# A decoder block on one core: four feed-forward products moved into the last attention batch, turns three units ahead

## The chip, the core and the metric

The kernel runs as one program on one core of a Trainium2 chip. TensorE (PE, with its weight loads listed apart as PEld), VectorE (DVE), ScalarE (ACT) and GpSimd (POOL) work side by side; SyncE (SP) issues the DMAs. Each engine takes its instructions in order, and the engines wait for one another by semaphores only. What counts is the device time of one execution in microseconds, as the median of several runs.

## What is computed

32 sequences of 56 tokens, 128 wide, pass through one decoder layer: linear self-attention, cross-attention (16 heads of 8) over a context of 1500 rows per sequence, and a feed-forward net, each with a residual and a layer norm. The change touches only the seam between cross-attention and feed-forward net:

```python
x = _layernorm(x + attn(x, ...))                    # LN1
x = _layernorm(x + xattn(x, ctx_1024, ctx_1024, ...))   # LN2, gives x2
hidden = x2 @ W1 + b1                               # 128 -> 512
imag   = w_imag * sin(theta + hidden * 0.1)
q      = hidden + (cos(theta)*w_real + sin(theta)*w_imag) * imag * 0.1
x = _layernorm(x2 + relu(q) @ W2 + b2)              # LN3
```

## The kernel before

The first 140 us hold the self-attention and the first norm. Then 32 batches of cross-attention follow (`body` on each engine), two to a pass of a loop, the last two written out by hand. A batch has 12 tiles of 125 context rows (`KT`), in six steps of two tiles, 2m and 2m+1. In a step PE multiplies queries and keys (`score`, line 1066, into banks 0 to 2, in turn by half tiles), ACT takes the exponential of each half (`exp`, line 756), and PE multiplies by the values (`pv`, lines 1083 and 1089, summed in bank 7). Between these, PE prepares the next batches (keys, values, row maxima) in four ring banks, 3 to 6. In the last batch (`not s2`) there is no next batch: the ring is empty but for `x2_T` in steps 2, 4 and 6 (by tile), which transposes the normed rows of quads 0 to 2 into bank 5, from where ACT copies them into `x2T` (line 830). A quad is 8 sequences, 512 columns.

The feed-forward net works in 16 units k, quad q = k // 4 by hidden slice g = k % 4, each 128 x 512 in float32. One unit passes through four engines:

- `hidden(k)`, PE line 1147: the product with W1, into bank g. It waits until `modulated(k - 4)` has read that bank (`z_ready`).
- `turn(k)`, ACT line 843: scale and bias, to turns of the sine, PSUM to SBUF.
- `rounded(k)`, DVE line 1446: the nearest whole number; then POOL line 696 subtracts it (the fraction).
- sine, ACT line 851 (behind one table load, since the last batch used the exponential).
- `modulated(k)`, DVE line 1452: sine times a coefficient plus the product in bank g; `relu(k)`, DVE line 1459; `project(k)`, PE line 1158: the product with W2.

The order on each engine is written out by hand. ACT: sine(k), then turn(k + AHEAD). DVE: modulated(k), rounded(k + AHEAD), relu(k), and between them the rest of the last pair of batches (`normalise_o` line 1336, `turn_o` line 1342, `add_y` line 1347, whose PE parts are the end units T line 982, Z line 986, Y line 989), the statistics and the norm of the last quad (`normalised(0, LAST)`, line 1394, behind the root on POOL, lines 542 and 545) and, at k = 6, 10 and 14, the sum and the statistics of a finished quad (`sum3`, lines 1465, 1379, 1385). PE: hidden(k), then project(k - 5). The turns, the whole numbers, the sines and the modulated values have four buffers each (`FBUF`). POOL does the 16 fractions in order, with the root of the last quad behind fraction 4 (`ROOT_UNIT`).

Before, no unit starts until the last exponential is through: PE waits for `p_ready` of all batches, then issues hidden(0), hidden(1). The lines that set this:

```python
AHEAD = 2
X2T_BANK, F_BANKS = banks[5], (banks[4], banks[7])
for k in range(AHEAD):
    turn(k)                                         # ACT, behind the last exponential
pe.wait_ge(p_ready, B * 2 * KT)                     # PE, ahead of hidden(0)
wait_past(pe, z_ready, k - G + 1)                   # in hidden(k): G = 4 banks
```

Of the kernel before, what the change touches and what calls it, by code (L numbers as in the profile page):

```python
# [33 lines left out]
ALU = mybir.AluOpType  # L34
# [3 lines left out]
P = 128  # L38
# [8 lines left out]
G = 4  # L47
# [39 lines left out]
def wait_past(engine, semaphore, count):  # L87

    if not isinstance(count, int) or count > 0:
        engine.wait_ge(semaphore, count)  # L90
# [10 lines left out]


STORE_ORDER = (0, 1, 3, 2)
END_SLOT = 3
END_UNITS = {2: "T", 4: "Z", 5: "Y"}
X2T_STEPS = (2, 4, 6)
FBUF = 4
PROJECT_LAG = 5
AHEAD = 2
ROOT_UNIT = 4  # L110
EARLY_M = 7
U1_SHIFT = 3
# [129 lines left out]
def decoder_block(nc, ctx_dram, x_dram, pack_dram, out_dram, m):  # L242
# [6 lines left out]
    with ExitStack() as stack:  # L249
# [112 lines left out]
        LAST = QUADS - 1  # L362
        W1, W2 = w("W1"), w("W2").rearrange("p (g n) -> p g n", g=G)
        out_view = out_dram.rearrange("(q p e) n d -> q e n p d", q=QUADS, e=2)
        X2T_BANK, F_BANKS = banks[5], (banks[4], banks[7])

        scores = banks[0:RING_AT]
        ring = banks[RING_AT:RING_AT + RING]
# [5 lines left out]
        with nc.Block() as block:  # L374
# [330 lines left out]
            def _(act):  # L705
# [121 lines left out]

                def x2_T(q):
                    act.wait_ge(x2T_ps, q + 1)
                    nc.scalar.copy(x2T[:, q, :], X2T_BANK).then_inc(x2T_sb, 1)  # L830

                for b in range(2):
                    body(b, b % 2, True, True)
# [6 lines left out]

                def turn(k):
                    act.wait_ge(h_ps, k + 1)
                    nc.scalar.activation(turns[:, k % FBUF, :], banks[k % G], ACT.Identity,
                                         bias=u_bias[:, k % G:k % G + 1], scale=0.1 * INV2PI).then_inc(turns_ready, 1)

                for k in range(AHEAD):
                    turn(k)
                for k in range(UNITS):
                    act.wait_ge(frac_ready, k + 1)
                    wait_past(act, z_ready, k - FBUF + 1)  # L850
                    nc.scalar.activation(sine[:, k % FBUF, :], turns[:, k % FBUF, :], ACT.Sin,
                                         scale=TWO_PI_BELOW).then_inc(sine_ready, 1)
                    if k + AHEAD < UNITS:
                        turn(k + AHEAD)
                    if k == ROOT_UNIT + 2:
                        x2_T(LAST)

            @block.tensor
            def _(pe):
# [197 lines left out]
                def score(b, t, u):  # L1057
                    if t == 0:
                        pe.wait_ge(k_stacked, (b + 1) * 96)
                        pe.wait_ge(qd_ready, b + 1)  # L1060
                        pe.wait_ge(m_placed, (b + 1) * 64)
                    wait_past(pe, p_ready, b * 2 * KT + 2 * t - 1)
                    for g in range(G):
                        for half in range(2):
                            rows = slice(HALF * half, HALF * half + HALF)
                            mm = nc.tensor.matmul(scores[(2 * t + half) % RING_AT][:, g * PAIR:(g + 1) * PAIR],  # L1066
                                                  k_stack[u][rows, g, t * KP:t * KP + P],
                                                  q_diag[u][rows, g * PAIR:(g + 1) * PAIR], start=True, stop=True)
                            if g == G - 1:
                                mm.then_inc(s_ready, 1)  # L1070
# [26 lines left out]
                def body(b, pair, u, s1, s2, before, held):  # L1097

                    held = dict(held)

                    def go(units):
                        for kind, i in units:
                            if active(kind, s1, s2, before):
                                n, slot = of_batch(kind, b, pair), slots[u][kind, i]
                                if kind in ("M1", "M2") and i in PAIRS:
                                    release(held[slots[u][kind, i + 1]])
                                unit(kind, i, n, u if kind in ("K2", "M2") else 1 - u, ring[slot], held[slot])
                                held[slot] = (kind, i, n)

                    for m, (one, two, three) in enumerate(plans[u]):  # L1110
                        score(b, 2 * m, u)
                        if not s2 and 2 * m in X2T_STEPS:
                            x2_T(X2T_STEPS.index(2 * m))
                        go(one)
                        score(b, 2 * m + 1, u)
                        go(two)
                        if m:
                            pv(b, 2 * m - 2, u)
                            pv(b, 2 * m - 1, u)
                        elif before:  # L1120
                            pv(b - 1, KT - 2, 1 - u)
                            pv(b - 1, KT - 1, 1 - u)
                        go(three)
                    if not s2:
                        pv(b, KT - 2, u)
                        pv(b, KT - 1, u)
# [6 lines left out]
                def x2_T(q):  # L1133

                    pe.wait_ge(x2_done, q + 1)
                    wait_past(pe, x2T_sb, q)
                    for p in range(4):
                        last = nc.tensor.transpose(X2T_BANK[:, p * P:(p + 1) * P], x_all[:, q, p * D:(p + 1) * D],
                                                   ident)
                    last.then_inc(x2T_ps, 1)  # L1140

                def hidden(k):
                    q, g = divmod(k, G)
                    if g == 0:
                        pe.wait_ge(x2T_sb, q + 1)
                    wait_past(pe, z_ready, k - G + 1)
                    nc.tensor.matmul(banks[g], W1[:, g * P:(g + 1) * P], x2T[:, q, :], start=True,
                                     stop=True).then_inc(h_ps, 1)

                def project(k):  # L1150
# [25 lines left out]
                pe.wait_ge(p_ready, B * 2 * KT)  # L1176
                for k in range(UNITS + PROJECT_LAG):
                    if k in END_UNITS:
                        unit(END_UNITS[k], 0, B // 2 - 1, 0, ring[END_SLOT], None)
                    if k == ROOT_UNIT + 5:  # L1180
                        x2_T(LAST)
                    if k < UNITS:
                        hidden(k)
                    if k >= PROJECT_LAG:
                        project(k - PROJECT_LAG)

            @block.vector
            def _(dve):
# [151 lines left out]
                def turn_o(pair, bank):  # L1340
                    dve.wait_ge(ready["Z"], pair + 1)
                    dve.tensor_copy(oT[:, :], bank[:, 0:P]).then_inc(oT_done, 1)
# [89 lines left out]
                with dve.Fori(1, B // 2 - 1) as i:  # L1432
                    for u in range(2):
                        body(i * 2 + u, i, u, True, True, True)
                body(B - 2, B // 2 - 1, 0, False, True, True)
                o_copy(B - 2, 0)
                invert_std(0, early, 1)
# [2 lines left out]
                body(B - 1, B // 2 - 1, 1, False, False, True)  # L1440


                def rounded(k):
                    dve.wait_ge(turns_ready, k + 1)
                    wait_past(dve, frac_ready, k - FBUF + 1)
                    dve.tensor_scalar(whole[:, k % FBUF, :], turns[:, k % FBUF, :], ROUND, -ROUND, ALU.add,
                                      ALU.add).then_inc(whole_ready, 1)

                def modulated(k):

                    dve.wait_ge(sine_ready, k + 1)
                    dve.scalar_tensor_tensor(z[:, k % FBUF, :], sine[:, k % FBUF, :], s_coef[:, k % G:k % G + 1],  # L1452
                                             banks[k % G], ALU.mult, ALU.add).then_inc(z_ready, 1)

                def relu(k):
                    dve.wait_ge(z_ready, k + 1)
# [5 lines left out]
                def sum3(q):  # L1462
# [5 lines left out]
                    stats_of(1, pairs)  # L1468
                    variances(1, pairs, q + 1)

                last_pair, last_quad = B // 2 - 1, range(4 * LAST, 4 * QUADS)
                o_copy(B - 1, 1)
                for k in range(AHEAD):
                    rounded(k)
                normalise_o(last_pair, ring[END_SLOT])
                for k in range(UNITS):
                    modulated(k)
                    if k + AHEAD < UNITS:
                        rounded(k + AHEAD)
                    relu(k)  # L1480
                    if k == 0:
                        turn_o(last_pair, ring[END_SLOT])
                    if k == 1:
                        add_y(last_pair, ring[END_SLOT])
                    if k == 2:
                        dve.wait_ge(y_added, last_pair + 1)
                        stats_of(0, last_quad)
                        variances(0, last_quad, 2)
                    if k == ROOT_UNIT:
                        invert_std(0, last_quad, 2)  # L1490
                        normalised(0, LAST).then_inc(x2_done, 1)
                    if k >= G + 2 and k % G == 2:
                        sum3(k // G - 1)
# [51 lines left out]
```

## Time and profile before

| what | us |
|---|---|
| median of 3 runs (lowest, highest) | 752.18 (751.29, 757.26) |
| the profiled execution | 756.2 |
| its span, first to last instruction | 754.4 |
| last batch and feed-forward net, from the last batch's first scores | 690.4 to 754.4 |

The profile shows one execution, 4.0 us above the median; its span is 1.8 us shorter than its time. Times of rows are microseconds from the span's start. A row of the timeline has start, duration, engine, line, operation, output <- inputs by the program's names, shapes and a count; in brackets stands how long the engine was idle before it and what ended that wait. A row of windows has the stretch, its length, the busy time of PE, PEld, DVE, ACT and POOL with instruction counts, the granted clock of TensorE as a share of 2.4 GHz, the share of the DMA engines and GB/s. The tiles have other names in the rows where memory is reused: `e_buf` holds the turns, `c_in` the whole numbers, the two `k_stack` the sines and the modulated values, `kf` is `x2T`, `qf` and `probs` take the results of `relu`, `pack` holds the weights.

### The profile page before, as it was taken

How to read it: one execution, taken by the hardware profiler on the slowest of the kernel's cores; microseconds unless marked ns; L12 is line 12 of the kernel's file. 1: busy time of each engine (PE TensorE's matmuls, PEld its weight loads, DVE VectorE, ACT ScalarE, POOL GpSimd, SP SyncE). 2: the span in 40 equal slices, each digit the busy share in tenths (PEclk: the TensorE clock that was granted, in tenths of full speed). 3: DMA queues.
4: the chain of work that ended last, by engine and by line, in shares of the span. 5: the costliest groups of instructions: out<-in, count | busy, mean ns of one | idle time of the engine just before them, and what ended most of it. 6: DMA issues, size and time to landing. Idle time of an engine off the chain costs nothing.

```text
span 754.4 us, 33172 instructions
## 1 busy us (share of the span) xinstructions
PE 677.6 (90%) x12468; PEld 436.7 (58%) x12468; DVE 586.4 (78%) x1139; ACT 549.5 (73%) x1123; POOL 470.6 (62%) x507
## 2 busy tenths in 40 slices
PE   6879865897899999999999999999999999997883
PEld 3556432554566666666666666666666666665552
DVE  3768866776687888888888887788888788885597
ACT  3537522786688888888888888888888888887751
POOL 6526424366467777777777767776777777723464
PEclk9989976799999999999999999999999999999997
DMA  7202502587758778888777877877787877851001
GB/s 215 82 2 93 95 1 65 82 161 171 146 120 161 147 144 151 158 161 176 149 146 157 152 151 152 151 151 143 149 159 166 170 150 144 140 108 21 1 1 49
DMA packets 39405, 93.20 MB, mean 124 GB/s; under 512 B 7880, under 2 KB 14536, under 8 KB 39368
## 3 DMA queue, kind: packets, MB, share of 16 engines
q1 hardware_dynamic: 39368, 92.69, 60.7%
q8 instruction: 25, 0.41, 0.3%
q14 instruction: 12, 0.10, 0.1%
HBM read 66.06 MB, written 26.54 MB: 123 GB/s over the span
## 4 chain that ended last, share of the span: by engine, by line
PE 68%; DVE 14%; issue 7%; ACT 6%; DMA 2%; SPq 1%; POOL 1%; ACTq 0%; DVEq 0%; POOLq 0%
PE psum L974 13%; PE psum L1066 13%; PE psum L1083 11%; PE psum L962 9%; PE psum L1089 8%; DVE mx L1313 4%; PE psum L954 4%; ACT probs L756 3%; PE psum L905 2%; DMA q_diag<-mT 1%; DVE rden L1241 1%; PE psum L891 1%; PE psum L920 1%; PE psum L982 1%; DVE k_stack L1452 1%
## 5 line engine op out<-in xcount | busy, mean ns | idle before, releaser
L1313 DVE TENSOR_REDUCE mx<-psum 128x1 f32<-128x500 f32 x672 | 424.3, 673 | 96.6 <-PE psum L974 94.5
L756 ACT ACTIVATE probs<-psum 125x448 f32<-125x448 f32 x768 | 376.2, 544 | 82.5 <-PE psum L1066 80.7
L974 PE MATMUL psum<-kh,q_max 64*128 64x500 f16 (+1 forms) x672 | 149.4, 385 | 12.5 <-DVE mx L1313 11.3
L1066 PE MATMUL psum<-q_diag,k_stack 64*128 64x112 f16 x3072 | 143.3, 212 | 12.6 <-issue 3.0
L1083 PE MATMUL psum<-probs,v_ext 125*32 125x112 f32 x3072 | 149.1, 266 | 0.0
L1089 PE MATMUL psum<-probs,v_ext 125*32 125x112 f32 x3072 | 144.3, 260 | 0.0
L580 POOL CAST kh<-k 128x500 f16<-128x500 f32 x96 | 57.7, 601 | 132.8 <-ACT k L776 125.1
L1066 PEld LDWEIGHTS psum<-q_diag,k_stack 64*128 64x128 f16 x3072 | 87.7, 95 | 88.2 <-ACT probs L756 50.5
L568 POOL TENSOR_TENSOR c_hl<-c_in,c_hl 128x500 f16<-128x500 f32 x96 | 109.9, 1145 | 7.7
L586 POOL TENSOR_TENSOR kl<-k,kh 128x500 f16<-128x500 f32 x96 | 107.3, 1146 | 0.0
L1083 PEld LDWEIGHTS psum<-probs,v_ext 125*32 125x32 f32 x3072 | 74.0, 109 | 35.9 <-issue 31.0
L1089 PEld LDWEIGHTS psum<-probs,v_ext 125*32 125x32 f32 x3072 | 87.2, 111 | 0.0
L566 POOL CAST c_hl<-c_in 128x500 f16<-128x500 f32 x96 | 59.4, 619 | 37.6 <-PE psum L962 35.2
L974 PEld LDWEIGHTS psum<-kh,q_max 64*128 64x128 f16 (+1 forms) x672 | 38.5, 94 | 67.4 <-issue 30.6
L962 PE MATMUL psum<-WvH,c_hl 128*128 128x128 f16 x768 | 76.0, 221 | 0.0
L962 PE MATMUL psum<-WvL,c_hl 128*128 128x128 f16 x384 | 69.8, 220 | 3.1 <-issue 3.1
L776 ACT ACTIVATE k<-psum,pack 128x500 f32<-128x500 f32 x96 | 65.1, 679 | 8.9 <-PE psum L954 7.6
L962 PEld LDWEIGHTS psum<-WvH,c_hl 128*128 128x128 f16 x768 | 58.2, 98 | 23.1 <-DVE mx L1313 15.4
L765 ACT COPY v_ext<-psum 125x512 f32<-125x512 f32 x96 | 56.4, 588 | 4.0 <-PE psum L962 4.0
L954 PE MATMUL psum<-c_hl,WkH 128*128 128x500 f16 x192 | 57.0, 378 | 0.4 <-ACT mT L771 0.4
L607 POOL TENSOR_TENSOR q_max<-qh,pack 128x896 f16<-128x896 f32 (+1 forms) x32 | 54.0, 1689 | 1.4 <-ACT qh L747 1.4
L726 ACT ACTIVATE e_buf<-psum 128x512 f32<-128x512 f32 x32 | 19.6, 611 | 28.4 <-PE psum L891 24.9
(143 smaller groups left out, 705.9 us busy)
## 6 DMA issues: line engine op xcount, KB each, us to landing
k_stack<-k_halves SPq DMA_DIRECT2D x192, 187.5 KB, 6.3
c_in<-ctx_in SPq DMA_DIRECT2D x32, 750.0 KB, 5.3
k_halves<-kh SPq DMA_DIRECT2D x32, 375.0 KB, 5.9
k_halves<-kl SPq DMA_DIRECT2D x32, 375.0 KB, 6.3
q_stack<-q_halves SPq DMA_DIRECT2D x32, 64.0 KB, 2.4
q_diag<-mT SPq DMA_DIRECT2D x64, 0.8 KB
q_diag<-mT SPq DMA_DIRECT2D x64, 0.1 KB
out<-x_all SPq DMA_DIRECT2D x8, 112.0 KB
```

Source lines behind the costliest of these rows:

```text
L566: nc.gpsimd.tensor_copy(c_hl[:, buf, 0, keys], c_in[:, buf, keys]).then_inc(c_hi, 1)
L568: nc.gpsimd.tensor_tensor(c_hl[:, buf, 1, keys], c_in[:, buf, keys], c_hl[:, buf, 0, keys], ALU.subtract).then_inc(c_split, 1)
L586: nc.gpsimd.tensor_tensor(kl[u][:, keys], k32[:, keys], kh[u][:, keys], ALU.subtract).then_inc(kl_done, 1)
L756: nc.scalar.activation(probs[0:KP, t % PBUF, half * 2 * GC:(half + 1) * 2 * GC], scores[k % RING_AT][0:KP, 0:2 * GC], ACT.Exp, scale=SCALE ...
L776: nc.scalar.activation(k32[:, i * CH:(i + 1) * CH], bank[:, 0:CH], ACT.Identity, bias=w("bk")).then_inc(k32_done, 1)
L954: last = nc.tensor.matmul(bank[:, 0:CH], wt[:, :], c_hl[:, u, part, i * CH:(i + 1) * CH], start=(k == 0), stop=(k == 2))
L962: last = nc.tensor.matmul(bank[:, j * P:(j + 1) * P], c_hl[:, u, part, at:at + P], wt[:, :], start=(k == 0), stop=(k == 2))
L974: last = nc.tensor.matmul(bank[:, 0:CH], q_max[u][rows, r * P:(r + 1) * P], kh[u][rows, c * CH:(c + 1) * CH], start=True, stop=True)
L1066: mm = nc.tensor.matmul(scores[(2 * t + half) % RING_AT][:, g * PAIR:(g + 1) * PAIR], k_stack[u][rows, g, t * KP:t * KP + P], q_diag[u][ro ...
L1083: nc.tensor.matmul(O[32 * j:32 * j + 32, 0:2 * N], v_ext[u][0:KP, v:v + 32], probs[0:KP, t % PBUF, at:at + 2 * N], start=(t == 0), stop=(t ...
L1089: last = nc.tensor.matmul(O[32 * j:32 * j + 32, 2 * N:GC], v_ext[u][0:KP, v:v + 32], probs[0:KP, t % PBUF, at + 2 * N:at + GC], start=Fals ...
L1313: dve.tensor_reduce(mx[:, r * KC + c:r * KC + c + 1], bank[:, 0:CH], AX.X, ALU.max).then_inc(mx_done, 1)
```

## The change

In the last batch PE now issues hidden(0) and hidden(1) in the step of tile 6, behind x2_T, hidden(2) in the step of tile 8 and hidden(3) in that of tile 10, each ahead of the step's second score. The products of all units go to the ring's banks 3 to 6 instead of banks 0 to 3. The turns of units 0 to 3 are made by DVE (`first_turn`) instead of ACT, each followed by its `rounded`, ahead of the last copy of O; POOL's order is as before, so its fractions 0 to 3 come as soon as those are there. In the rest of the net a turn runs three units ahead of its sine instead of two. The transposes of the last quad, the results of `project` and the end units move to other banks.

```diff
-END_SLOT = 3
-AHEAD = 2
+AHEAD = 3
+PREPARED = 4
+PREPARED_AT = {6: (0, 1), 8: (2,), 10: (3,)}
...
-        X2T_BANK, F_BANKS = banks[5], (banks[4], banks[7])
+        X2T_BANKS, F_BANKS, END_BANK = (banks[5], banks[2]), (banks[0], banks[1]), banks[7]
...
-                    nc.scalar.activation(turns[:, k % FBUF, :], banks[k % G], ACT.Identity,
+                    nc.scalar.activation(turns[:, k % FBUF, :], banks[3 + k % G], ACT.Identity,
...
-                for k in range(AHEAD):
-                    turn(k)
                 for k in range(UNITS):
...
-                    if k + AHEAD < UNITS:
+                    if PREPARED <= k + AHEAD < UNITS:
                         turn(k + AHEAD)
...
                         go(one)
+                        if not s2 and 2 * m in PREPARED_AT:
+                            for k in PREPARED_AT[2 * m]:
+                                hidden(k)
                         score(b, 2 * m + 1, u)
...
-                        unit(END_UNITS[k], 0, B // 2 - 1, 0, ring[END_SLOT], None)
+                        unit(END_UNITS[k], 0, B // 2 - 1, 0, END_BANK, None)
...
-                    if k < UNITS:
+                    if PREPARED <= k < UNITS:
                         hidden(k)
...
+                def first_turn(k):
+                    dve.wait_ge(h_ps, k + 1)
+                    dve.tensor_scalar(turns[:, k, :], banks[3 + k % G], 0.1 * INV2PI, u_bias[:, k % G:k % G + 1],
+                                      ALU.mult, ALU.add).then_inc(turns_ready, 1)
...
+                for k in range(PREPARED):
+                    first_turn(k)
+                    rounded(k)
                 last_pair, last_quad = B // 2 - 1, range(4 * LAST, 4 * QUADS)
                 o_copy(B - 1, 1)
-                for k in range(AHEAD):
-                    rounded(k)
-                normalise_o(last_pair, ring[END_SLOT])
+                normalise_o(last_pair, END_BANK)
                 for k in range(UNITS):
                     modulated(k)
-                    if k + AHEAD < UNITS:
+                    if PREPARED <= k + AHEAD < UNITS:
                         rounded(k + AHEAD)
                     relu(k)
```

PE in the last batch, from x2_T of quad 2 (line 1138) to the score of tile 8, before. Line 1066 is a score of one tile, lines 1083 and 1089 are products with the values.

```order
L1138 MATMUL psum<-pack,x_all 128x128 x4
L1066 MATMUL psum<-q_diag,k_stack 128x112 x8
L1083 MATMUL psum<-probs,v_ext 32x112 x4
L1089 MATMUL psum<-probs,v_ext 32x112 x4
L1083 MATMUL psum<-probs,v_ext 32x112 x4
L1089 MATMUL psum<-probs,v_ext 32x112 x4
L1066 MATMUL psum<-q_diag,k_stack 128x112 x16
```

The same place in the changed kernel, whose lines there are x2_T 1140, hidden 1149, score 1065, pv 1082 and 1088:

```order
L1140 MATMUL psum<-pack,x_all 128x128 x4
L1149 MATMUL psum<-kf,pack 128x512 x2
L1065 MATMUL psum<-q_diag,k_stack 128x112 x8
L1082 MATMUL psum<-probs,v_ext 32x112 x4
L1088 MATMUL psum<-probs,v_ext 32x112 x4
L1082 MATMUL psum<-probs,v_ext 32x112 x4
L1088 MATMUL psum<-probs,v_ext 32x112 x4
L1065 MATMUL psum<-q_diag,k_stack 128x112 x8
L1149 MATMUL psum<-kf,pack 128x512
L1065 MATMUL psum<-q_diag,k_stack 128x112 x8
```

Two products stand between x2_T and the score of tile 7, and one between the two scores of the next step.

DVE behind the norm of quads 0 to 2 (line 1394), before: the copy of O (1351), two roundings (1446), the reciprocal and the product of `normalise_o`, then modulated(0) (1452), rounded(2), relu(0) (1459), the copy for Y (1342), modulated(1).

```order
L1394 TENSOR_SCALAR x_all<-x_all,mv_f,rstd_f 128x128 x12
L1351 COPY o_sb<-psum 128x4x56
L1446 TENSOR_SCALAR c_in<-e_buf 128x512 x2
L1329 RECIPROCAL r_tok<-psum 128x16
L1336 TENSOR_TENSOR o_tok<-psum,r_tok 128x2x4x8 x2
L1452 SCALAR_TENSOR_TENSOR k_stack<-k_stack,s_coef,psum 128x512
L1446 TENSOR_SCALAR c_in<-e_buf 128x512
L1459 TENSOR_SCALAR qf<-k_stack,pack 128x512
L1342 COPY oT<-psum 128x128
L1452 SCALAR_TENSOR_TENSOR k_stack<-k_stack,s_coef,psum 128x512
```

The same place in the changed kernel, from the last first_turn (1445) and its rounded (1440), of which three more such pairs stand ahead:

```order
L1445 TENSOR_SCALAR e_buf<-psum,u_bias 128x512
L1440 TENSOR_SCALAR c_in<-e_buf 128x512
L1353 COPY o_sb<-psum 128x4x56
L1331 RECIPROCAL r_tok<-psum 128x16
L1338 TENSOR_TENSOR o_tok<-psum,r_tok 128x2x4x8 x2
L1459 SCALAR_TENSOR_TENSOR k_stack<-k_stack,s_coef,psum 128x512
L1466 TENSOR_SCALAR qf<-k_stack,pack 128x512
L1344 COPY oT<-psum 128x128
L1459 SCALAR_TENSOR_TENSOR k_stack<-k_stack,s_coef,psum 128x512
L1440 TENSOR_SCALAR c_in<-e_buf 128x512
```

The roundings 0 to 3 now stand ahead of the copy of O, and rounded(4) stands directly behind modulated(1), one unit earlier than before.

## Rows read from the trace of the kernel before

**Rows 1.** The page's busy time of each engine, share of the span, instructions.

```profile
PE 677.6 (90%) x12468; PEld 436.7 (58%) x12468; DVE 586.4 (78%) x1139; ACT 549.5 (73%) x1123; POOL 470.6 (62%) x507
```

**Rows 2.** Windows: the seam, units 0 to 4, units 5 to 15.

```profile
703.20:708.40 5.20, 4.79 (x37) 2.29 (x29) 2.55 (x7) 3.34 (x5) 1.95 (x2) 1.00 0.00 0
708.40:720.10 11.70, 9.12 (x46) 5.92 (x45) 11.67 (x30) 7.47 (x13) 8.87 (x8) 1.00 0.00 1
720.10:744.90 24.80, 18.97 (x114) 14.22 (x114) 22.86 (x58) 10.59 (x18) 16.97 (x12) 0.99 0.00 1
```

**Rows 3.** Timeline of the last batch: scores, products with values, exponentials, then hidden(0), hidden(1).

```profile
697.15 0.37 PE L1066 MATMUL psum<-q_diag,k_stack 64*128 64x112 f16 x8
...
697.88 3.02 ACT L756 ACTIVATE probs<-psum 125x448 f32<-125x448 f32 x6
...
699.51 0.37 PE L1066 MATMUL psum<-q_diag,k_stack 64*128 64x112 f16 x8 [0.63 <-ACT probs L756]
...
699.82 0.40 PE L1083 MATMUL psum<-probs,v_ext 125*32 125x112 f32 x8
...
700.72 0.37 PE L1066 MATMUL psum<-q_diag,k_stack 64*128 64x112 f16 x8
701.13 1.98 ACT L756 ACTIVATE probs<-psum 125x448 f32<-125x448 f32 x4 [0.23 <-PE psum L1066]
...
703.70 1.98 PE L1147 MATMUL psum<-kf,pack 128*128 128x512 f32 x4
```

**Rows 4.** Timeline of the seam.

```profile
703.84 0.39 DVE L1351 COPY o_sb<-psum 128x224 f32<-128x224 f32 x1 [8.81 <-PE psum L1089]
...
704.86 0.69 ACT L843 ACTIVATE e_buf<-psum,u_bias 128x512 f32<-128x512 f32 x1 [1.75 <-PE psum L1147]
...
705.52 0.60 PE L982 MATMUL psum<-pack,o_sb 128*128 128x128 f32 x4
...
706.42 1.28 ACT L851 ACT_TABLE_LOAD   x1
...
707.55 0.25 DVE L1329 RECIPROCAL r_tok<-psum 128x16 f32<-128x16 f32 x1
...
707.72 0.63 ACT L851 ACTIVATE k_stack<-e_buf 128x512 f32<-128x512 f32 x1
707.84 0.35 DVE L1336 TENSOR_TENSOR o_tok<-psum,r_tok 128x64 f32<-128x64 f32 x2
...
708.38 0.75 DVE L1452 SCALAR_TENSOR_TENSOR k_stack<-k_stack,s_coef,psum 128x512 f32<-128x512 f32 x1 [0.19 <-ACT k_stack L851]
```

**Rows 5.** Timeline: a rounding while POOL stands still, then one full unit.

```profile
725.68 0.42 DVE L1446 TENSOR_SCALAR c_in<-e_buf 128x512 f32<-128x512 f32 x1
...
728.33 0.75 DVE L1452 SCALAR_TENSOR_TENSOR k_stack<-k_stack,s_coef,psum 128x512 f32<-128x512 f32 x1
...
728.99 0.73 DVE L1446 TENSOR_SCALAR c_in<-e_buf 128x512 f32<-128x512 f32 x1
...
729.64 0.47 DVE L1459 TENSOR_SCALAR qf<-k_stack,pack 128x512 f32<-128x512 f32 x1
729.80 1.45 POOL L696 TENSOR_TENSOR e_buf<-e_buf,c_in 128x512 f32<-128x512 f32 x1 [0.36 <-DVE c_in L1446]
```

**Rows 6.** Timeline: POOL's root and fractions 5 and 6, DVE's norm of the last quad.

```profile
714.77 0.23 POOL L542 TENSOR_SCALAR std_f<-mv_f 128x4 f32<-128x4 f32 x1 [0.15 <-DVE mv_f L1385]
...
716.09 1.27 POOL L696 TENSOR_TENSOR e_buf<-e_buf,c_in 128x512 f32<-128x512 f32 x1
...
717.72 1.44 POOL L696 TENSOR_TENSOR e_buf<-e_buf,c_in 128x512 f32<-128x512 f32 x1 [0.36 <-DVE c_in L1446]
...
717.96 2.06 DVE L1394 TENSOR_SCALAR x_all<-x_all,mv_f,rstd_f 128x128 f32<-128x128 f32 x4
```

**Rows 7.** Windows of the net's end, and a float32 product of 128 x 512 at 0.50.

```profile
744.00:746.00 2.00, 0.54 (x5) 0.33 (x3) 1.09 (x5) 0.00 (x0) 0.87 (x1) 0.59 0.00 0
...
130.03 2.07 PE L940 MATMUL psum<-x1T,pack 128*128 128x512 f32 x2 [0.68 <-ACT x1T L743]
```

More of the change, by code:

```diff
@@ L829, in x2_T @@
                     act.wait_ge(x2T_ps, q + 1)
-                    nc.scalar.copy(x2T[:, q, :], X2T_BANK).then_inc(x2T_sb, 1)
+                    nc.scalar.copy(x2T[:, q, :], X2T_BANKS[q // LAST]).then_inc(x2T_sb, 1)
                 for b in range(2):
@@ L1137, in x2_T @@
                     for p in range(4):
-                        last = nc.tensor.transpose(X2T_BANK[:, p * P:(p + 1) * P], x_all[:, q, p * D:(p + 1) * D],
-                                                   ident)
+                        last = nc.tensor.transpose(X2T_BANKS[q // LAST][:, p * P:(p + 1) * P],
+                                                   x_all[:, q, p * D:(p + 1) * D], ident)
                     last.then_inc(x2T_ps, 1)
@@ L1146, in hidden @@
                     wait_past(pe, z_ready, k - G + 1)
-                    nc.tensor.matmul(banks[g], W1[:, g * P:(g + 1) * P], x2T[:, q, :], start=True,
+                    nc.tensor.matmul(banks[3 + g], W1[:, g * P:(g + 1) * P], x2T[:, q, :], start=True,
                                      stop=True).then_inc(h_ps, 1)
@@ L1434, in _, with rounded @@
                         body(i * 2 + u, i, u, True, True, True)
+                def rounded(k):
+                    dve.wait_ge(turns_ready, k + 1)
+                    wait_past(dve, frac_ready, k - FBUF + 1)
+                    dve.tensor_scalar(whole[:, k % FBUF, :], turns[:, k % FBUF, :], ROUND, -ROUND, ALU.add,
+                                      ALU.add).then_inc(whole_ready, 1)
+                def first_turn(k):
+                    dve.wait_ge(h_ps, k + 1)
+                    dve.tensor_scalar(turns[:, k, :], banks[3 + k % G], 0.1 * INV2PI, u_bias[:, k % G:k % G + 1],
+                                      ALU.mult, ALU.add).then_inc(turns_ready, 1)
                 body(B - 2, B // 2 - 1, 0, False, True, True)
@@ L1440, in _ @@
                 body(B - 1, B // 2 - 1, 1, False, False, True)
[L1443 to L1447, printed above, removed]
                 def modulated(k):
@@ L1452, in modulated @@
                     dve.scalar_tensor_tensor(z[:, k % FBUF, :], sine[:, k % FBUF, :], s_coef[:, k % G:k % G + 1],
-                                             banks[k % G], ALU.mult, ALU.add).then_inc(z_ready, 1)
+                                             banks[3 + k % G], ALU.mult, ALU.add).then_inc(z_ready, 1)
                 def relu(k):
@@ L1481, in _ @@
                     if k == 0:
-                        turn_o(last_pair, ring[END_SLOT])
+                        turn_o(last_pair, END_BANK)
                     if k == 1:
-                        add_y(last_pair, ring[END_SLOT])
+                        add_y(last_pair, END_BANK)
                     if k == 2:
```

## The prediction

> **What bounds the kernel now.** I read the busy times first: PE leads with 90% of the span, DVE follows with 78% [rows 1]. That average says little here, since the change touches only the last 64 us. So I cut that stretch into windows [rows 2]. In the seam, from the last exponential to the first modulated unit, DVE works 2.55 of 5.20 us and POOL 1.95: everybody waits in turn. In units 0 to 4 DVE is busy for 11.67 of 11.70 us, and in units 5 to 15 for 22.86 of 24.80, most of the rest being one wait for a root at the end. So the last batch is an ACT matter, the seam a chain of latencies, the net a DVE matter.
>
> In the last batch, ACT runs six exponentials without a gap (697.88, 3.02 us), then four more after a wait of 0.23 [rows 3]. A step of two tiles takes it 1.98 + 0.23 = 2.21 us. PE in the same step gives 0.31 us to each score (699.51 to 699.82) and 0.90 to the values of two tiles (699.82 to 700.72): 1.52 us, so 0.69 us are spare.
>
> The seam is read along the waits [rows 4]. The last exponential ends at 703.11 (701.13 + 1.98). hidden(0) is issued at 703.70, its turn starts 1.16 us later, the second turn follows, then the table load at 706.42, the first sine at 707.72 and modulated(0) at 708.38, which the row says waited for that sine. From the last exponential to modulated(0) that is 5.27 us.
>
> A steady unit [rows 5]: modulated 0.75, rounded 0.73, relu 0.47, and POOL's fraction 1.45 us, starting 0.36 after the one before it ended, so every 1.81 us. The rounding takes 0.42 us when POOL stands still, and 0.73 when a fraction runs: it ends only when POOL has finished. This ring (fraction, then the next rounding, then the next fraction) sets 1.81 us, not DVE's own sum, 0.67 + 0.35 + 0.40 = 1.42 us from start to start with the starts overlapped by some 0.08.
>
> **The change part by part.** *Products in the last batch.* Four rows of line 1147, two products, start at 703.70 and the next PE work starts at 705.52 [rows 3, 4]: 0.91 us each. Two of them stand ahead of the score of tile 7, which was issued at 697.15. It moves to 698.97, and an exponential starts 0.41 us behind its score (700.72 to 701.13), so at 699.38. That exponential started at 697.88 before: 1.50 us late. In each of the next two steps PE now has 1.52 + 0.91 = 2.43 us against ACT's 2.21, 0.22 each. Sum: +1.9 us at the last exponential. Bounds: 0, if PE's spare time hides all of it, and 4 x 0.91 = 3.6, if none. I take 1.9, since it is the sum of steps that rows show.
>
> *The seam.* The turns of units 0 to 3 move to DVE, which waits 8.81 us ahead of the copy of O [rows 4]. A read of PSUM by DVE on this shape costs about what modulated does, 0.75 [rows 5]: 4 x (0.75 + 0.42) = 4.7 us, hidden by that wait, and the four fractions by an idle POOL. Without that cover the fourth pair would push the copy of O by 1.2 us. Behind the last exponential two chains remain. ACT: table load 1.28 and sine 0.63, 1.96 us with the small gaps. DVE and PE: the copy of O starts 0.73 after the exponential and takes 0.39, then T 0.60, the reciprocal 0.25, the product 0.35, with some 0.05 for each of four hand-overs: 2.5 us. The second ends last, so 5.27 becomes 2.5: -2.75 us. What is late next is the old rest of the attention, no longer the table load.
>
> One rule bears on this. In the row the sine starts 0.02 us after the table load has ended (706.42 + 1.28 = 707.70, then 707.72) [rows 4]. The Trainium skill (page "ScalarE: Activation LUTs", section "What ACT_TABLE_LOAD costs") adds a drain of about 1.38 us to each switch, 2.66 us in all. By the row ACT's chain is 1.96 us and hidden; by the rule it would be 3.34 and set the end, +0.85 on the sum. The trace shows no drain, so I go by the row and keep the rule as a rival.
>
> *Units 0 to 4, with turns three ahead.* DVE loses two roundings here, at 0.42 that is -0.84. But the turns gain a tighter loop. There are still four banks, so hidden(k + 3) waits for modulated(k - 1), where hidden(k + 2) waited for modulated(k - 2). From the end of modulated(0) to rounded(4): 0.1 for the hand-over, 1.16 to the turn, 0.69 for the turn [rows 4], 1.95 us in all. DVE has only relu(0), the copy for Y and modulated(1) meanwhile, 0.40 + 0.20 + 0.67 = 1.27 (the copy is an estimate from that of O, 0.39 for 224 columns [rows 4], at 128): it stands for 0.7 us in front of rounded(4), with relu(1) and all behind it, and much the same in front of rounded(7). POOL then adds to it. The root of the last quad stands behind fraction 4 and needs the statistics that DVE makes behind relu(2). With modulated(0) at 708.38 - 2.75 + 1.9 = 707.5, rounded(4) starts at 710.2, and relu(1), add_y, modulated(2), rounded(5), relu(2) and the statistics follow until 714.1. Then POOL does the root in 1.32 (714.77 to 716.09 [rows 6]) and fractions 5, 6 and 7, all of them waiting, at about 1.3, 1.3 and 1.45, until 719.5. Before, only two fractions stood ahead of the norm: fraction 6 ended at 719.16 and the norm at 720.02, 0.86 later. With one more the norm ends at about 720.4 to 720.7. I take 720.5: from modulated(0) this stretch grows from 11.65 to 13.0 us, +1.35. Bounds: -0.84, if nobody ever waits for a turn, and +2.5, if each of the turns 4 to 7 costs 0.7 and the roundings go at no gain.
>
> *Units 5 to 15.* In the steady stretch the new loop takes 1.95 + 0.42 + 0.40 + 0.67 = 3.44 us for two units, 1.72 each, under POOL's 1.81: nothing. Behind each of the first two sums, where POOL is idle and DVE could run a unit in 1.4 us, the loop costs some 0.2: +0.4. At the end the last rounding comes one unit earlier: -0.2. Sum +0.2. Bounds: -0.4, and +3.6 (the second rival).
>
> *Other banks, other places of the end units.* T, Z and Y now work in bank 7 and wait for the copy of O as before; project finds banks 0 and 1 free, since sine(0) follows the last exponential on ACT. No queue has a DMA moved. 0, with the sum of the seam as cover.
>
> **Sum.** 1.9 - 2.75 + 1.35 + 0.2 = +0.7 us. The profiled execution, 754.4 us of span and 756.2 in all, would become 755.1 and 756.9. It lies 4.0 us above the median of the runs, in what no part of this change touches, so I add the difference to the median: 752.18 + 0.7 = 752.9 us. A measurement of this kernel can tell about 1%, 7.5 us, from no change, so I expect a result that cannot be told from it.
>
> **The rivals.** *The head start stays.* If the turns three ahead never hold DVE, the gain of the seam remains: 1.9 - 2.75 - 0.84 - 0.4 = -2.1, 750.1 us. For it: in the steady unit POOL's ring, not the turn, decides. Against it: four banks, and a chain of 1.95 us where DVE has 1.27 to do.
>
> *The slower side: hidden stands behind project.* PE takes its products in order. If hidden(k + 3) regularly finds project(k - 3) just started, it waits up to 0.9 us more, the chain grows from 1.95 to 2.85 and a unit to (2.85 + 1.49) / 2 = 2.15 us against 1.81. Over 11 units that is +3.6, 756.5 us. It decides from the point where relu and modulated free the two products at the same moment. Against it: project of a unit is released four units earlier, so it normally runs right behind the hidden before it.
>
> *The clock falls in the seam.* The granted clock fell towards 0.50, 1.2 GHz, at 744 to 746, with PE busy for 0.54 of 2 us [rows 7]. With four products gone, PE has little but T, Z and Y for some 2.5 us. A float32 product of this shape took 2.07 at 0.50 [rows 7], against 1.0 in the net; two units of hidden and project slower by some 1.8 each would be +3.6, 756.5. Against it: the clock was 1.00 through the stretch with similar pauses in units 0 to 4 [rows 2].
>
> *The drain of the page.* +0.85 more: 753.8. *The change does not do what it says:* the prepared units are not finished when the batch ends, so that the 1.9 us remain and about half of the seam's gain goes: 754.3.
>
> **How the numbers follow.** Forecast 0.55, head start 0.18, project 0.12, clock 0.07, drain 0.04, not prepared 0.04. The range is 749.5 to 757.0: the low end is the first rival less 0.6 us for the scatter of runs, the high end the second and third with 0.5 more. The forecast's own range is 751.5 to 755. None of the cases is 1% faster, 744.7: 0.02. Project and clock together would reach 760, over 759.7: 0.04. Within 1%: 0.94.
>
> **What would show it.** Right: the last exponential ends some 1.9 us later, with the gap in front of the exponentials of tile 7; the table load follows the last exponential at once; modulated(0) starts about 2.5 us behind it, waiting for the product of normalise_o; DVE stands some 0.7 us in front of rounded(4), by ACT's turn; three fractions run without a pause behind the root. Wrong: no wait for turns in units 4 to 7, roundings at 0.42 in the steady units, units longer than 1.81 us, or a granted clock under 1.00 between 705 and 740.

## The result: one part in a hundred slower by the medians, two microseconds slower where the change works

The changed kernel took 764.91 us, median of 5 runs (758.77 to 765.63), against 757.26 for 5 runs of the kernel before: the 3 shown above and two more, 762.66 and 1824.48. The ratio is 1.0111 with an interval of 1.0065 to 1.0157. The ratios here and below leave out runs over 1.5% above the fastest of their kernel, with them some of the plain scatter (4 of 12 runs of e3_ahead2, 1 of 12 of e2_after_again), while the medians hold all runs. Forecast were 752.9 us, in a range of 749.5 to 757.0. The profiled execution took 758.77 us, its span 757.0, 2.6 us more than before.

The two traces allow a sharper comparison. Take the copy of O of the batch before the last as zero (DVE line 1351 before, 1353 after, at 690.51 and 691.15): it lies ahead of everything that the change touches. From there to the end of DVE's last instruction it is 61.05 us before and 62.98 after, **+1.93 us**. The other 0.64 us of the spans' difference arose earlier, where the change edits nothing.

The last batch after, from the timeline (lines 1149 hidden, 757 exponentials; compare [rows 3]):

```profile
697.08 0.66 PE L1140 MATMUL psum<-pack,x_all 128*128 128x128 f32 x4
697.58 1.88 PE L1149 MATMUL psum<-kf,pack 128*128 128x512 f32 x4
...
699.39 0.37 PE L1065 MATMUL psum<-q_diag,k_stack 64*128 64x112 f16 x8
...
699.80 0.98 ACT L757 ACTIVATE probs<-psum 125x448 f32<-125x448 f32 x2 [1.16 <-PE psum L1065]
...
702.36 0.98 ACT L757 ACTIVATE probs<-psum 125x448 f32<-125x448 f32 x2 [0.38 <-PE psum L1065]
...
704.93 0.98 ACT L757 ACTIVATE probs<-psum 125x448 f32<-125x448 f32 x2 [0.38 <-PE psum L1065]
```

The score of tile 7 stands behind two products, and ACT waits 1.16 us for it; behind each of the later two products ACT waits 0.38 us. The last exponential ends at 705.91 (704.93 + 0.98), 2.16 us later against the zero point than before.

The seam, of the same timeline (compare [rows 4]):

```profile
705.93 1.28 ACT L850 ACT_TABLE_LOAD   x1
...
706.64 0.39 DVE L1353 COPY o_sb<-psum 128x224 f32<-128x224 f32 x1 [0.79 <-PE psum L1088]
...
707.17 0.63 PE L981 MATMUL psum<-pack,o_sb 128*128 128x128 f32 x4 [0.60 <-DVE o_sb L1353]
707.22 1.15 ACT L850 ACTIVATE k_stack<-e_buf 128x512 f32<-128x512 f32 x2
...
708.13 0.35 DVE L1338 TENSOR_TENSOR o_tok<-psum,r_tok 128x64 f32<-128x64 f32 x2
708.40 0.74 DVE L1459 SCALAR_TENSOR_TENSOR k_stack<-k_stack,s_coef,psum 128x512 f32<-128x512 f32 x1
```

From the last exponential to modulated(0) it is now 2.49 us instead of 5.27. The sines are ready early; the copy of O, T and normalise_o decide.

Units 1 to 4, of the same timeline (compare [rows 6]):

```profile
711.14 0.43 DVE L1440 TENSOR_SCALAR c_in<-e_buf 128x512 f32<-128x512 f32 x1 [0.62 <-ACT e_buf L844]
...
715.06 0.23 POOL L543 TENSOR_SCALAR std_f<-mv_f 128x4 f32<-128x4 f32 x1 [1.96 <-DVE mv_f L1387]
...
716.38 4.12 POOL L697 TENSOR_TENSOR e_buf<-e_buf,c_in 128x512 f32<-128x512 f32 x3
...
717.54 0.43 DVE L1440 TENSOR_SCALAR c_in<-e_buf 128x512 f32<-128x512 f32 x1 [0.54 <-ACT e_buf L844]
...
717.88 1.50 DVE L1466 TENSOR_SCALAR probs<-k_stack,pack 128x512 f32<-128x512 f32 x1
...
719.30 2.05 DVE L1396 TENSOR_SCALAR x_all<-x_all,mv_f,rstd_f 128x128 f32<-128x128 f32 x4
```

DVE waits 0.62 us in front of rounded(4) and 0.54 in front of rounded(7), both for ACT's turn. POOL stands still for 1.96 us in front of the root, then does three fractions in a row, 4.12 us, and DVE's relu(4) takes 1.50 instead of 0.48 beside them; the norm takes 2.05, as before. The norm ends at 721.35, 12.95 us behind modulated(0), where it was 11.64.

Then the clock. From the windows after (the columns as in [rows 2], the granted clock third from the end), and the timeline:

```profile
718.00:720.00 2.00, 1.42 (x10) 0.99 (x8) 2.00 (x2) 1.53 (x3) 2.00 (x2) 1.00 0.00 0
720.00:722.00 2.00, 0.59 (x4) 0.42 (x4) 2.00 (x6) 0.00 (x0) 0.50 (x1) 0.95 0.00 0
722.00:724.00 2.00, 2.00 (x4) 0.91 (x4) 1.40 (x4) 0.00 (x0) 1.44 (x1) 0.50 0.00 0
724.00:726.00 2.00, 2.00 (x11) 1.76 (x10) 1.10 (x3) 1.69 (x3) 0.60 (x1) 0.70 0.04 8
```

```profile
722.06 2.07 PE L1149 MATMUL psum<-kf,pack 128*128 128x512 f32 x2
...
724.17 0.69 ACT L844 ACTIVATE e_buf<-psum,u_bias 128x512 f32<-128x512 f32 x1 [4.40 <-PE psum L1149]
...
724.89 0.43 DVE L1440 TENSOR_SCALAR c_in<-e_buf 128x512 f32<-128x512 f32 x1 [1.50 <-ACT e_buf L844]
```

PE was busy for 0.59 of 2 us while the norm of the last quad ran. Then the granted clock is 0.50, 1.2 GHz, from about 722 to 725. hidden(9) takes 2.07 instead of 1.1 us, its turn comes late, and DVE stands for 1.50 us in front of rounded(9). Before, hidden(9) ran at 720.73, and the clock was 1.00:

```profile
720.00:722.00 2.00, 1.93 (x9) 1.21 (x10) 2.00 (x6) 0.99 (x2) 0.91 (x1) 1.00 0.00 0
...
720.73 1.13 PE L1147 MATMUL psum<-kf,pack 128*128 128x512 f32 x2
```

### The profile page after: what moved, and what is told of

The parts are those of the page before. It is cut to its first block, busy times and chain, and to the rows that moved or that the text cites. A ratio compares the mean times of both kernels' runs of the same rounds, so it can differ in the third digit from the quotient of the medians.

```text
span 757.0 us, 33172 instructions
## 1 busy us (share of the span) xinstructions
PE 681.2 (90%) x12468; PEld 438.3 (58%) x12468; DVE 588.7 (78%) x1143; ACT 547.7 (72%) x1119; POOL 470.5 (62%) x507
## 4 chain that ended last, share of the span: by engine, by line
PE 70%; DVE 13%; issue 7%; ACT 6%; DMA 2%; SPq 1%; POOL 0%; ACTq 0%; DVEq 0%; POOLq 0%
PE psum L973 13%; PE psum L1065 13%; PE psum L1082 11%; PE psum L961 9%; PE psum L1088 8%; DVE mx L1315 5%; PE psum L953 4%; ACT probs L757 3%; PE psum L904 2%; PE psum L1149 2%; PE psum L890 1%; DVE rden L1243 1%; DMA q_diag<-mT 1%; PE psum L981 1%; PE psum L888 1%
```

## The experiments

All were timed in later sessions; where a ratio is given, it is against runs of the kernel before in the same comparison. The distances are differences of timeline rows of each profile, from the copy of O of the batch before the last (zero) to the end of the last exponential, the start of modulated(0), the end of the last quad's norm, the start of the first sum (k = 6) and the end of DVE's work, in us.

| kernel | last exponential | modulated(0) | norm | first sum | end |
|---|---|---|---|---|---|
| before | 12.60 | 17.87 | 29.51 | 32.63 | 61.05 |
| e1_before_again | 12.59 | 17.87 | 29.50 | 32.61 | 61.04 |
| after | 14.76 | 17.25 | 30.20 | 34.48 | 62.98 |
| e2_after_again | 14.75 | 17.24 | 30.19 | 34.47 | 62.96 |
| e3_ahead2 | 14.76 | 17.25 | 28.00 | 31.12 | 59.54 |
| e4_fill | 14.75 | 17.24 | 30.19 | 33.53 | 62.02 |
| e5_five_banks | 14.76 | 17.25 | 29.52 | 32.64 | 60.67 |
| e6_root_later | 14.77 | 17.26 | 29.21 | 32.54 | 61.01 |
| e7_prep2_ahead2 | 13.30 | 15.79 | 27.77 | 30.89 | 59.32 |
| e8_before_ahead3 | 12.59 | 19.21 | 32.90 | 36.36 | 64.84 |
| e9_prep3_ahead2 | 13.89 | 16.38 | 27.57 | 30.68 | 59.12 |
| e10_five_root | 14.76 | 17.25 | 28.51 | 31.62 | 59.64 |

**Both kernels again.** No edit.

> The kernel before, unchanged, timed against itself. Theory A (the scatter of runs carries most of the 7.65 us between the two medians; the change itself costs about 2 us, as the two profiles show from the last batch on): the interval of the ratio holds 1.000 and is some 0.005 wide or more on each side. Theory B (the change costs 7 to 8 us in most executions, which the one profile, the fastest of its runs, does not show): the ratio is 1.000 within 0.003, so that 1.011 cannot be scatter.

> The changed kernel, unchanged, once more. Theory A: ratio near 1.002 to 1.004, and from the last batch's first score to the end of DVE again about 63.1 us against 61.2. Theory B: ratio near 1.011 again, and in a slower execution a longer net, by a granted clock under 1.00 in more of it than 721.9 to 725.3. My theory before the result (turns three ahead eat the gain of the seam): the last exponential 2.2 us late, modulated(0) 2.5 us behind it, the stretch from there to the norm's end 12.9 us.

Measured: the kernel before against itself 1.0021 (0.9983 to 1.0059), median 758.68 of 12 runs; the changed kernel 1.0000 (0.9965 to 1.0034), median 759.2 of 12 runs, beside 758.33 for 35 runs of the kernel before, which lie between 752.15 and 764.19. Theory B falls with the second of these: the 1.011 of the first comparison did not come back. The first alone does not decide, since 1.0021 also lies within the 0.003 that theory B named. Theory A holds in that both intervals contain 1.000; they are a little narrower than it said, 0.0034 to 0.0038 to each side instead of 0.005, and 1.0000 is less than its 1.002 to 1.004. Its distances hold: two profiles of one kernel agree within 0.02 us over the last 61 to 63 us. Whether a slower execution has a longer net was not seen, since both profiles show quicker ones, 755.12 and 756.02 us. The ratio 1.0000 says less than it seems, since the interval is some 5 us wide; +1.93 us lies within it.

Where the scatter arises is seen in the distances between the copies of O of successive batches. From the fourth on they are 17.87 and about 17.1 us in turn, with few exceptions, up to the last one ahead of the zero point, which lies between 16.91 and 18.81. The first three were 18.65, 19.73 and 19.24 us in e10_five_root (749.09 us) and 19.38, 24.27 and 23.58 in e6_root_later (762.58 us). Their sum runs from 57.62 to 67.23 us over the twelve profiles; the first copy, ahead of them, comes at 153.34 to 157.52. Two windows and a PE row from the third of these distances, e10 first:

```profile
200.00:205.00 5.00, 2.99 (x60) 1.86 (x59) 2.17 (x5) 3.49 (x8) 3.14 (x4) 1.00 0.64 86
205.00:210.00 5.00, 4.83 (x120) 3.46 (x121) 3.68 (x6) 3.85 (x8) 2.00 (x3) 1.00 0.64 152
...
204.93 0.27 PE L963 MATMUL psum<-WvH,c_hl 128*128 128x128 f16 x2 [1.89 <-issue]
```

```profile
200.00:205.00 5.00, 2.96 (x67) 2.00 (x63) 3.08 (x6) 2.38 (x5) 3.47 (x4) 1.00 1.03 138
205.00:210.00 5.00, 2.90 (x19) 1.12 (x19) 0.78 (x2) 1.61 (x3) 0.00 (x0) 0.50 0.07 13
...
207.09 0.46 PE L1065 MATMUL psum<-q_diag,k_stack 64*128 64x112 f16 x5 [4.13 <-issue]
```

In the last row PE has stood for 4.13 us in the middle of a score. "issue" means that the profile shows nothing that it waited for; DVE and ACT wait for PE, for 4.99 and 4.83 us, POOL does nothing from 205 to 210, and PE goes on at a clock of 0.50. From 150 to 225 us such pauses of PE come to 4.7 us in e10 and to 10.4 in e6, and all twelve profiles have them. No part of the change is near. What makes PE pause, and longer in some executions than in others, was not tried and stays open.

**Turns two ahead.**

```diff
-AHEAD = 3
+AHEAD = 2
```

> The changed kernel with turns two ahead, as before; the four products stay in the last batch. If the loop of the turns is what eats the gain: from modulated(0) to the norm's end about 10.3 us, not 12.95, no wait of DVE in front of rounded(4) and rounded(7), the norm before the third waiting fraction; in all 2.5 to 3.5 us under the changed kernel and 1 to 2 us under the kernel before, ratio about 0.998. Rival (the loss comes from the products in the last batch and the clock, not from the turns): within 1 us of the changed kernel, and the clock falls at the same place.

Measured: 59.54, 3.44 us under the changed kernel and 1.51 under the kernel before; modulated(0) to the norm 10.75 us; median 754.21, ratio 0.9918 (0.9876 to 0.9960), of which the traces support 0.998. The rows of e3 where the changed kernel waited:

```profile
709.23 0.42 DVE L1440 TENSOR_SCALAR c_in<-e_buf 128x512 f32<-128x512 f32 x1
...
711.33 0.23 POOL L543 TENSOR_SCALAR std_f<-mv_f 128x4 f32<-128x4 f32 x1 [0.16 <-DVE mv_f L1387]
...
712.65 1.27 POOL L697 TENSOR_TENSOR e_buf<-e_buf,c_in 128x512 f32<-128x512 f32 x1
...
714.29 1.44 POOL L697 TENSOR_TENSOR e_buf<-e_buf,c_in 128x512 f32<-128x512 f32 x1 [0.36 <-DVE c_in L1440]
714.52 2.06 DVE L1396 TENSOR_SCALAR x_all<-x_all,mv_f,rstd_f 128x128 f32<-128x128 f32 x4
```

rounded(4) waits for nothing, two fractions stand between root and norm, and the clock stays at 1.00. So the turns three ahead, not the products in the last batch, cost the gain. The stretch came out 0.45 us longer than expected.

**PE kept busy in front of the transposes.** The two products' results are not used.

```diff
+FILL = 2
...
                     if k == ROOT_UNIT + 5:
+                        for _ in range(FILL):
+                            nc.tensor.matmul(X2T_BANKS[1], W1[:, 0:P], x2T[:, 0, :], start=True, stop=True)
                         x2_T(LAST)
```

> The changed kernel with two more products of 128 x 512 on PE in front of the transposes of the last quad, into a bank that these overwrite; their results are not used. If the pause of PE in front of the norm's end makes the clock fall: clock 1.00 from 720 to 726, hidden(9) at about 1.1 instead of 2.07 us, DVE's wait in front of rounded(9) down from 1.50 to some 0.5, 1 us gained from the norm's end on. Theory B in addition: the median falls by several us. Rival (the clock does not depend on this pause): hidden(9) again at 2.07, and no gain.

Measured: 62.02, 0.96 us less than the changed kernel, nearly all of it between norm and first sum (3.34 instead of 4.28 us). Windows of e4, and its rounded(9):

```profile
720.00:722.00 2.00, 1.74 (x7) 0.71 (x6) 2.00 (x7) 0.00 (x0) 0.08 (x1) 1.00 0.00 0
722.00:724.00 2.00, 2.00 (x12) 1.34 (x11) 1.45 (x4) 1.19 (x3) 1.45 (x1) 1.00 0.00 0
```

```profile
723.53 0.43 DVE L1443 TENSOR_SCALAR c_in<-e_buf 128x512 f32<-128x512 f32 x1 [0.55 <-ACT e_buf L845]
```

The clock is 1.00 and the wait 0.55, so the slow clock's price here is 0.96 us. The median did not fall (761.29, ratio 1.0033, 0.9997 to 1.0070), the last of theory B.

**Five banks; the root later; both.** Five banks for the products, so that hidden waits for one unit further back (turn, first_turn and modulated read the same five, and the transposes of the last quad go to bank 7); in the second kernel, only POOL's root one fraction later; in the third both.

```diff
+        H_BANKS = (banks[3], banks[4], banks[5], banks[6], banks[2])
...
-                    wait_past(pe, z_ready, k - G + 1)
-                    nc.tensor.matmul(banks[3 + g], W1[:, g * P:(g + 1) * P], x2T[:, q, :], start=True,
+                    wait_past(pe, z_ready, k - 5 + 1)
+                    nc.tensor.matmul(H_BANKS[k % 5], W1[:, g * P:(g + 1) * P], x2T[:, q, :], start=True,
...
-                    if k == ROOT_UNIT:
+                    if k == ROOT_UNIT + 1:
                         root_f(0, 4 * LAST, 4 * QUADS, 2)
```

> The changed kernel, turns three ahead, with five banks for the products of the units (3 to 6 and 2; the transposes of the last quad go to bank 7), so that hidden(k + 3) waits for modulated(k - 2). If the missing bank makes the loop: no wait of DVE in front of rounded(4) and rounded(7) on ACT's turn, the clock or not; from modulated(0) to the norm's end 12.5 us instead of 12.95, and about 1 us less in all (not counting the clock's 0.96), so that some 2 us of the distance to turns two ahead stay: they are the order itself (three fractions in front of the norm). Rival (the wait for the bank explains all of the distance): 10.8 us to the norm's end, as with turns two ahead.

> The changed kernel with POOL's root of the last quad behind fraction 5 instead of fraction 4. If the fractions that pile up behind the root hold the norm: fraction 5 runs while DVE makes the statistics, two fractions instead of three stand between root and norm, the stretch from modulated(0) to the norm's end falls from 12.95 to about 12.0 us. Rival (the root comes later by one fraction and the norm with it): 12.9 us or more.

> The changed kernel, turns three ahead, with both five banks and the root behind fraction 5. If the two causes of the loss are the missing bank and the fractions behind the root: from modulated(0) to the norm's end 11.2 us, about 1.0 less than with five banks alone, in all 59.6 us from the copy of O to DVE's end, as with turns two ahead (59.54). Rival (turns three ahead cost something else too): 60.5 us or more, the gain of the two edits not adding up.

Measured: five banks 60.67, 1.35 us under e4_fill, which like it has no slow clock in front of the first sum; the norm 12.27 us behind modulated(0), and no wait in front of rounded(4), but still the three fractions:

```profile
711.13 0.43 DVE L1442 TENSOR_SCALAR c_in<-e_buf 128x512 f32<-128x512 f32 x1
...
716.38 4.08 POOL L698 TENSOR_TENSOR e_buf<-e_buf,c_in 128x512 f32<-128x512 f32 x3
```

Root later: 61.01, 1.01 us under e4_fill, the norm 11.95 us behind modulated(0); POOL no longer waits in front of the root, and one fraction less stands behind it:

```profile
720.84 0.23 POOL L543 TENSOR_SCALAR std_f<-mv_f 128x4 f32<-128x4 f32 x1 [0.15 <-DVE mv_f L1387]
...
722.16 1.27 POOL L697 TENSOR_TENSOR e_buf<-e_buf,c_in 128x512 f32<-128x512 f32 x1
```

Both: 59.64. 1.35 + 1.01 = 2.36, and e4_fill less this kernel is 2.38: the two causes add up and leave 0.10 us to turns two ahead. Up to the norm this kernel is 0.51 us behind turns two ahead (11.26 against 10.75 us), since four roundings stand there instead of three; behind the first sum, with one rounding less, it takes 28.02 us against 28.42. With the clock the 3.44 us are settled: bank 1.35, fractions behind the root 1.01, clock 0.96, and 0.1 besides. The bank came dearer than the 1 us expected of it.

**Turns three ahead alone.** The kernel before, with one edit.

```diff
-AHEAD = 2
+AHEAD = 3
```

> The kernel before with turns three ahead and nothing else. If turns three ahead are what costs: modulated(0) 1.3 to 1.5 us later, since one more turn and rounding stand in front of it, and the stretch to the norm's end some 1.3 us longer; in all about 3 us more from the last batch on. Rival (turns three ahead are harmless without the products in the last batch): within 0.5 us of the kernel before.

Measured: 64.84, +3.79 us; modulated(0) 1.34 later, the stretch to the norm 13.69 instead of 11.64. Part is the clock again, granted at 0.63 in 715 to 718 and at 0.54 in 731 to 733; its share was not taken apart. So turns three ahead also cost some 3.8 us without the products in the last batch, but not in the same places: the 1.34 us in front of modulated(0), where one more turn and rounding stand, do not arise in the changed kernel.

**Fewer products in the last batch, turns two ahead.**

```diff
-AHEAD = 3
-PREPARED = 4
-PREPARED_AT = {6: (0, 1), 8: (2,), 10: (3,)}
+AHEAD = 2
+PREPARED = 2
+PREPARED_AT = {8: (0,), 10: (1,)}
```

and, for e9, 3 with {6: (0,), 8: (1,), 10: (2,)}.

> Only two products in the last batch, one each in the steps of tiles 8 and 10; turns two ahead. If each product behind its score costs PE's spare time first: the last exponential 0.4 to 0.8 us late instead of 2.16, modulated(0) 2.5 us behind it; then the stretch to the norm's end is about 12.1 us, since DVE does two roundings more there; in all 1.5 to 2 us under the kernel before from the last batch on, about the same as four products with turns two ahead. Rival (the late last exponential is the whole cost): 1.4 us better than four products with turns two ahead.

> Three products in the last batch, one each in the steps of tiles 6, 8 and 10; turns two ahead. The last exponential 1.2 to 1.4 us late, modulated(0) 2.5 us behind it, 11.2 us from there to the norm's end (one rounding more on DVE than with four products, one less than with two). In all within 0.3 us of two and of four products with turns two ahead, 59.2 to 59.5 us from the copy of O to DVE's end: each product moved costs in the last batch what it saves in the net. Rival (there is a best number in between): under 58.9 us. Ratio to the kernel before about 0.993 to 0.997.

Measured: 59.32 and 59.12, so with four products (59.54) all within 0.42 us and 1.5 to 1.9 us under the kernel before. The last exponential comes 0.70 and 1.29 us late. Medians 754.89 (0.9931, 0.9892 to 0.9970) and 758.2 (1.0008, 0.9959 to 1.0057): the two kernels differ by 0.2 us in the trace and by 3.3 in the medians, which come from two sessions and show again what a median of this kernel can tell. The ratio expected of three products, 0.993 to 0.997, did not come. Three products with turns two ahead beat both kernels by the trace; by the medians nothing can be said of it.

## Why the prediction was right or wrong

**The number was wrong**, 764.91 against a range that ended at 757.0. The step that failed is "so I add the difference to the median", with the 0.5 to 0.6 us that the range allowed for scatter. The median of three runs was no fixed point: 35 later runs of the same kernel had a median of 758.33, 6.15 us higher, and reached 764.19. The measured median was no fixed point either: 12 later runs of the changed kernel had 759.2, 5.7 us under the 764.91. Beside the 758.33 that is +0.9 us, near the forecast's +0.7, but with an interval of some 2.6 us to each side this confirms nothing. Most of the scatter arises in the first three batches.

**The sum was too small**, +0.7 against +1.93, term by term:

- Products in the last batch: forecast +1.9, measured +2.16. The two places are right, the sizes less so: the exponential of tile 7 comes 1.28 us late, where 1.50 was expected, and each later product adds 0.44, where 0.22 was. Two products in a row take PE 0.91 us each, as forecast, but a single one takes 1.06, from 700.90 to the score at 701.96:

```profile
700.90 1.13 PE L1149 MATMUL psum<-kf,pack 128*128 128x512 f32 x2
701.96 0.37 PE L1065 MATMUL psum<-q_diag,k_stack 64*128 64x112 f16 x8
```

- Seam: forecast -2.75, from 5.27 to 2.5; measured 2.49, -2.78. The chain over normalise_o decides, as said, and the turns on DVE are hidden (0.75 us each).
- The drain: no run shows it. The sine starts at 707.22, 0.01 behind the end of the load at 707.21. The Trainium skill (page "ScalarE: Activation LUTs", section "What ACT_TABLE_LOAD costs") and the measurement differ, and the measurement decides.
- Units 0 to 4: forecast +1.35, measured 12.95 less 11.64, +1.31. Both causes named were there, 0.62 us in front of rounded(4) and three fractions behind the root, and e5, e6 and e10 tell them apart.
- Units 5 to 15: forecast +0.2, measured 32.78 less 31.54, +1.24. This is the term that was mis-sized. 0.96 of it is the clock, the third rival, which had 0.07 and stood in no term of the sum; it came, and at the norm of the last quad rather than between the end units, and at a quarter of its price. A granted clock under 1.00 between 705 and 740 was named as a sign of being wrong. The rest, 0.28, is as forecast.
- hidden behind project, 3.6 us: did not come. POOL's fractions of the steady stretch started 2.02, 1.81 and 1.81 us apart (728.69 to 734.33), against 1.81 before. The roundings took 0.43 to 0.54 us there, near the 0.42 that was named as a sign of being wrong: DVE now waits 0.55, 0.27 and 0.22 us for the turn in front of them, where it was held up by POOL before, and only the first of these waits lengthens the unit. The rival's price was also added wrongly: (2.85 + 1.49) / 2 is 2.17, which over 11 units makes +4.0 and not +3.6.

**The rival "the head start stays"**, -2.1, did not come, since the turns did hold DVE. The kernel nearest to it is the one with turns two ahead: -1.51 measured.

## What to carry to other kernels

Running a stage further ahead was no gain here while the banks behind it stayed as many: the wait moved to the next product, which cost 1.35 us, and one more fraction stood in front of the norm, which cost 1.01. Compare short stretches of two traces from a point ahead of the change; here they agree within 0.02 us, while medians move by several us for reasons far from it. A change that thins out PE's work can cost something by the clock too, 0.96 us here, so look at the granted clock behind such a place.

## What the runs showed that was not expected

The clock fell in both profiles of the changed kernel, behind the norm, and twice in that of e8, in the seam and behind the norm. It did not fall in e5, where PE stood still for 3.31 us in front of the same transposes, against 1.98 in the changed kernel:

```profile
720.00:722.00 2.00, 0.63 (x5) 0.63 (x6) 2.00 (x6) 0.00 (x0) 0.46 (x1) 1.00 0.00 0
...
721.37 0.66 PE L1142 MATMUL psum<-pack,x_all 128*128 128x128 f32 x4 [3.31 <-DVE x_all L1398]
```

So the length of the pause alone does not tell whether it falls. In e5 PE was busier ahead of the pause, without a gap from 712 to 718, where the changed kernel had 4.95 of 6 us; whether that is the reason was not tried.

And a float32 subtraction on POOL held up DVE's relu: relu(4), begun at 717.88 while a fraction ran, took 1.50 us instead of 0.48. The statistics took 0.86 us at 713.41 in the kernel before, beside a fraction (713.17 to 714.62), and 0.86 at 713.70 in the changed one, with POOL idle.
